# Counting edges with (destination, source parity) on the partitions: narrower one-hots, three-byte unpacking and another ScalarE order

## The chip, the cores and the metric

The kernel runs on one core of a Trainium2 chip. The metric is the device time of one execution in microseconds (us). Engines are named as in the profile: PE is TensorE's matmul side, PEld its weight loads, DVE VectorE, ACT ScalarE, POOL GpSimd, SP SyncE, which here only issues DMAs. A name with a q (DVEq) is the sequencer of an engine: it works on registers and semaphores and passes instructions on to the engine.

## The reference

A graph network over 6250 nodes and 100,000 edges sorted by destination, and then an expert FFN:

```python
n = x.shape[0]
deg = segment_sum(ones(rows.shape), rows, num_segments=n) + 1.0
dinv = rsqrt(deg)[:, None]
h = x @ W_in + b_in                      # x here is the layernorm of the input, 6250 x 256
for l in range(4):
    h_scaled = h * dinv
    msg = segment_sum(h_scaled[cols], rows, num_segments=n) * dinv
    global_ctx = mean(h, axis=0) @ Wg[l] + bg[l]
    z = relu((h + msg) @ Wl[l] + bl[l] + global_ctx)
    h = (z - mean(z)) * rsqrt(var(z) + EPS) * gamma[l] + beta[l]
...
x = x + h;  x = x + ffn(layernorm(x))    # top 2 of 8 experts
```

## The kernel before

The nodes lie in T = 49 tiles of 128. The edges are never gathered: the kernel first builds the dense matrix of edge counts (49 x 49 blocks of 128 x 128, as fp8) and writes it to HBM; each of the four layers then multiplies it with the node table. Building the matrix is the **counting stage**, the only one that the change touches. It goes through 49 **columns** m, one for each tile of 128 destinations. The edges lie in blocks of 128, sorted by destination, so a column needs only a window of WIN = 18 blocks.

For one column the engines do this:

- DVE writes one **source one-hot** for each block (`hots`, L724): a row of WP = 540 values for each edge, 49 tiles x 11 lanes, holding at the right place a power of four (which of 12 groups of 11 sources the edge falls in, so that one count word packs 12 two-bit counts). Two columns share 35 of them. It also writes the **destination one-hots** of the next column in one instruction (`hot_rows`, L708; `relative`, L699 and L700, prepares them from a start that is loaded into a register), the layernorm statistics of one tile of x (L731 to L747), and, once ACT has extracted the count words of the column before, the four **masks** that split them into two-bit fields (`mask`, L757).
- PE multiplies destination and source one-hots (`counts`, L1286, in two halves of 270 since 540 exceed one PSUM bank), and in between for the column before: `turn` (transpose of the normalised x tile), `product` (times W_in), `degrees` (49 matmuls of one column over the unpacked bytes, L1266) and `add_mean` (L1310).
- ACT copies the transposed tile (xnT, L1108), **unpacks** the masks into fp8 bytes with 12 ACTIVATEs (L1094), normalises the next x tile (xnb, L1112), stores h0 (L1100) and copies the count **words** out of PSUM (L1118).
- SP writes four finished columns at a time to HBM.

Each engine runs its list strictly in order; semaphores join them. Count words have two PSUM banks each and two buffers, the masks one. All names with `tab`, `later` and `region` in the profile are views of three big SBUF buffers.

## Time and profile before

| | us |
|---|---|
| median of 3 runs (3206.35 to 3207.5) | 3206.64 |
| the profiled execution | 3210.56 |
| its span, first to last instruction | 3208.6 |
| busy: PE / DVE / ACT / POOL | 3076.7 / 1901.3 / 855.9 / 70.3 |
| mean granted TensorE clock | 0.975 |

The span has five parts: setup (0 to 40 us), the counting stage (40 to 506), a change-over in which the counts are checked and the node table is made (506 to 563), the four layers (563 to 2806) and the FFN (2806 to the end). An engine's busy share says nothing by itself, since the stages are bound differently.

### The profile page before, as it was taken

Reading aid. Unit: us, or ns where it says so; the run is one execution under the profiler, and the core shown is the slowest. Engines: PE = TensorE matmul, PEld = TensorE weight load, DVE = VectorE, ACT = ScalarE, POOL = GpSimd, SP = SyncE. Lnnn points to the kernel's source line nnn. Section 1 sums busy time; section 2 is a strip of 40 time slices with the busy share of each in tenths; the row PEclk is TensorE's granted clock in tenths of the full one; section 3 lists DMA queues with packets and bytes.
Section 4 is the critical chain, followed back from the end, with each engine's and each line's share of the span. In section 5 each row is a group of like instructions: output and inputs, shape, how many; then the busy total and the mean of one; then the engine's idle time right before and its main releaser. Section 6 shows DMA issues by size and latency. Waiting matters only on the chain.

```text
span 3208.6 us, 54202 instructions
## 1 busy us (share of the span) xinstructions
PE 3076.7 (96%) x17323; PEld 1804.0 (56%) x17323; DVE 1901.3 (59%) x5185; ACT 855.9 (27%) x1934; POOL 70.3 (2%) x168
## 2 busy tenths in 40 slices
PE   6999996999999999999999999999999999979998
PEld 4777773444444444444444444444444444468887
DVE  8999997555555545555554555555566666645554
ACT  4989896111111111111111111111111111132332
POOL 0000000000000000000000000000000000001010
PEclk9989996999999999999999999999999999989999
DMA  4323324122222222222222222222222222110000
GB/s 130 96 83 94 91 82 122 61 70 70 70 70 70 70 70 70 70 70 70 70 70 70 70 70 70 70 70 70 80 82 82 82 82 82 48 40 16 18 18 18
DMA packets 134110, 225.11 MB, mean 70 GB/s; under 512 B 12277, under 2 KB 106596, under 8 KB 134018
## 3 DMA queue, kind: packets, MB, share of 16 engines
q1 hardware_dynamic: 131666, 217.53, 20.9%
q0 software_dynamic: 2352, 6.40, 0.8%
q8 instruction: 52, 0.85, 0.1%
q14 instruction: 40, 0.33, 0.0%
HBM read 178.17 MB, written 45.74 MB: 70 GB/s over the span
## 4 chain that ended last, share of the span: by engine, by line
PE 84%; ACT 9%; DVE 3%; issue 2%; DMA 1%; SPq 0%; DVEq 0%; ACTq 0%; POOLq 0%; POOL 0%
PE bank L1416 64%; ACT tab L1094 7%; PE bank L1490 5%; PE bank L1496 5%; PE bank L1374 4%; PE bank L1364 1%; PE bank L1266 1%; PE bank L1286 1%; DVE later L757 1%; DMA tab<-in_x 1%; DVE region L724 1%; PE bank L1310 1%; ACT later L1118 0%; PE bank L1304 0%; ACT xnb L1112 0%
## 5 line engine op out<-in xcount | busy, mean ns | idle before, releaser
L1416 PE MATMUL bank<-tab,region 128*128 128x512 f16 x9604 | 2143.2, 380 | 14.3 <-DVE tab L840 14.0
L1416 PEld LDWEIGHTS bank<-tab,region 128*128 128x128 fp8e4 x9604 | 940.8, 98 | 1065.5 <-DVE tab L840 17.9
L1094 ACT ACTIVATE tab<-later 128x539 fp8e4<-128x539 uint8 x588 | 336.1, 674 | 1.9 <-DVE later L757 1.9
L724 DVE TENSOR_SCALAR region<-iota_w,src_col,src_w 128x540 bf16<-128x540 int16 x858 | 310.8, 415 | 0.4 <-issue 0.3
L941 DVE SCALAR_TENSOR_TENSOR region<-bank,c_back,later 128x256 f32<-128x256 f32 x196 | 94.8, 484 | 351.2 <-PE bank L1374 351.2
L1197 ACT ACTIVATE sd<-mv,eps_c 128x1 f32<-128x1 f32 x196 | 57.8, 295 | 817.6 <-DVE mv L948 817.6
L936 DVE TENSOR_TENSOR region<-bank,region 128x256 f16<-128x256 f32 x196 | 83.3, 425 | 287.7 <-ACT region L1193 287.7
L1193 ACT ACTIVATE region<-bank 128x256 f16<-128x256 f32 x196 | 75.3, 384 | 568.2 <-PE bank L1364 568.2
L1490 PE MATMUL bank<-tab 128*128 128x384 f32 (+1 forms) x544 | 178.0, 487 | 3.8 <-DMA b_s<-in_L_ffn_b 3.8
L1496 PE MATMUL bank<-tab 128*128 128x256 f32 (+1 forms) x784 | 175.5, 384 | 0.9 <-ACT tab L1221 0.9
L1490 PEld LDWEIGHTS bank<-tab 128*128 128x128 f32 x544 | 164.4, 310 | 13.4 <-issue 6.3
L1374 PE MATMUL bank<-later,region 128*128 128x256 f16 x1176 | 161.0, 273 | 0.9 <-DVE region L936 0.9
L1496 PEld LDWEIGHTS bank<-tab 128*128 128x128 f32 (+1 forms) x784 | 148.8, 192 | 22.3 <-ACT tab L1221 1.4
L1191 ACT ACTIVATE region<-bank 128x256 f32<-128x256 f32 x196 | 75.3, 384 | 294.0 <-PE bank L1416 294.0
L1161 ACT ACTIVATE tab<-region,c_write 128x256 f32 x147 | 74.6, 508 | 274.1 <-DVE region L957 274.1
L1374 PEld LDWEIGHTS bank<-later,region 128*128 128x128 f16 x1176 | 115.2, 98 | 56.3 <-DVE region L936 1.2
L1221 ACT ACTIVATE tab<-bank,b_s 128x384 f32<-128x384 f32 (+1 forms) x136 | 77.2, 568 | 249.3 <-PE bank L1490 249.3
L1286 PE MATMUL bank<-region 128*128 128x270 bf16 x900 | 131.0, 299 | 1.3 <-DVE region L708 0.8
L1286 PE MATMUL bank<-region,later 128*128 x864 | 129.3, 309 | 1.4 <-DVE region L724 1.4
L925 DVE TENSOR_TENSOR region<-bank,region 128x256 f32<-128x256 f32 x196 | 83.0, 423 | 73.9 <-ACT region L1191 73.9
L1286 PEld LDWEIGHTS bank<-region,later 128*128 128x128 f16 x864 | 112.7, 145 | 15.4 <-issue 2.5
L1286 PEld LDWEIGHTS bank<-region 128*128 128x128 f16 x900 | 108.7, 146 | 19.9 <-DVE region L724 1.8
(199 smaller groups left out, 2232.8 us busy)
## 6 DMA issues: line engine op xcount, KB each, us to landing
region<-adjacency SPq DMA_DIRECT2D x196, 784.0 KB, 4.3
adjacency<-tab SPq DMA_DIRECT2D x12, 3136.0 KB, 13.7
region<-in_x POOLq DMA_DIRECT2D x48, 128.0 KB, 2.3
out<-region SPq DMA_DIRECT2D x48, 128.0 KB, 1.7
tab<-in_x SPq DMA_DIRECT2D x1, 6016.0 KB
tab<-in_L_ffn_W SPq DMA_DIRECT2D x4, 512.0 KB, 4.7
region<-in_L_gnn_Wl SPq DMA_DIRECT2D x1, 1024.0 KB, 5.4
later<-in_L_gnn_Wg SPq DMA_DIRECT2D x1, 1024.0 KB, 9.4
```

The costliest lines, as they stand in the source:

```text
L724: v.tensor_scalar(hot_s[:, j, :], iota_w[:, 0:WP], src_col[:, ds(first_block[0] + j, 1)], src_w[:, ds(first_block[0] + j, 1)], ALU.is_equa ...
L925: tile_own.done(v.tensor_tensor(acc_s, acc[a][:, 0:D], lo_f[:, a, :], ALU.add))
L936: v.tensor_tensor(uT[:, 1, :, :], T3[3], uT[:, 0, :, :], ALU.subtract).then_inc(uT_split, 1)
L941: tile_own.done(v.scalar_tensor_tensor(out=Z, in0=bank[4][:, 0:D], scalar=c_back[:, ds(n, 1)], in1=bias[:], op0=ALU.mult, op1=ALU.add))
L1094: ins = a.activation(stage[h][:, :, slot, f * LANES:f * LANES + n], counts[:, :, 0:n], ACT.Copy, saturate=False)
L1191: a.activation(lo_f[:, s, :], acc[s][:, D:2 * D], ACT.Copy).then_inc(lo_ready, 1)
L1221: a.activation(gT[:, f, 0:w], bank[f % 3][:, 0:w], ACT.Gelu, bias=b1_s[:, f // FC, f % FC:f % FC + 1]).then_inc(gelu_done, 1)
L1286: ins = mm(bank[k % 2 * 2 + half][:, 0:HALFP], hot_d[m % 2][:, :, j], hot_s[:, block + j, half * HALFP:(half + 1) * HALFP], start=j == 0, ...
L1374: ins = mm(bank[4][:, 0:D], uT[:, a, k, :], Wx[:, b, l, k, :], start=q == 0, stop=q == len(parts) - 1)
L1416: ins = mm(acc[a][:, :], A_s[:, a, m, :], tab[:, here + m, :], start=m == 0, stop=m == T - 1)
L1490: ins = mm(bank[f % 3][:, 0:w], W1_s[:, f // FC * KC + k, f % FC:FF:FC], xfT[:, k, 0:w], start=k == 0, stop=k == KC - 1)
L1496: ins = mm(bank[5 + u][0:r, 0:D], gT[:, f, u * P:u * P + r], W2_s[:, f // FC, f % FC, :], start=f == 0, stop=f == TOP * FC - 1)
```

## The change

A tile of 128 partitions of a count block now stands for 64 destinations times the parity of the source's tile (partition 2 x (destination in the half tile) + parity). A source one-hot therefore distinguishes 25 tile pairs instead of 49 tiles: 276 values instead of 540. A column is counted as two parts e = 0, 1 of 64 destinations each with a window of 10 blocks (20 matmuls of 275 instead of 36 of 270); four parts (two columns) form a group that shares 35 one-hots, as before. The destination one-hots grow from 18 to 20 blocks. `relative` loads two starts instead of one. The masks cover 1100 values instead of 1080. The unpacking takes three bytes in one ACTIVATE (five instead of twelve, 6400 elements instead of 6272). ACT works one column at once (words, xnT, root, normalise the next tile, unpack 0 and 1, h0, unpack 2 and 3), statistics are made two tiles ahead and their root and reciprocal for two tiles at a time, `degrees` comes two columns behind, and the masks follow the fourth one-hot of a column instead of the seventh. SP writes a group of columns with four DMAs of half the partitions and half the tiles. Words, masks and destination one-hots moved from `later` to `region`; the layer weights got buffers of their own. In the diff the old bodies of functions that are printed above are left out.

```diff
-WIN = 18
-STEP_LO, STEP_HI = 13, 17
-SLOTS = STEP_HI + WIN
-PAIRS = T // 2
-COLS = -(-NB // WIN) * WIN
+HALF_WIN = 10
+WIN = 2 * HALF_WIN
+HP = P // 2
+GROUP = 4
+GROUPS = -(-2 * T // GROUP)
+STEP_LO, STEP_HI = -2, 1
+STEP = HP * NE // (N * P)
+SLOTS = (GROUP - 1) * STEP + STEP_HI + HALF_WIN
+COLS = -(-(NB + SLOTS - HALF_WIN) // WIN) * WIN
...
-HALFP = WP // 2
+TI = -(-T // 2)
+WP = TI * LANES
+WS = -(-WP // 4) * 4
...
+words_w = work(4 * WP)
+words = words_w.bitcast(I32).rearrange("p (a s) -> p a s", a=2)
+words16 = words_w.bitcast(U16).rearrange("p (a s) -> p a s", a=2)
+masked_w = work(8 * WP)
+masked8 = masked_w.bitcast(U8).rearrange("p (k q s b) -> p k q b s", k=4, s=LANES, b=4)
...
-    sp.dma_start(X[:, 0, :], x[0:P, :]).then_inc(x0_in, 16)
-    sp.dma_start(X[:, 1:T - 1, :], x[P:(T - 1) * P, :].rearrange("(t p) f -> p t f", p=P)).then_inc(x_in, 16)
+    sp.dma_start(X[:, 0:2, :], x[0:2 * P, :].rearrange("(t p) f -> p t f", p=P)).then_inc(x0_in, 16)
+    sp.dma_start(X[:, 2:T - 1, :], x[2 * P:(T - 1) * P, :].rearrange("(t p) f -> p t f", p=P)).then_inc(x_in, 16)
...
     def write(h, m0, width):
         sp.wait_ge(staged, m0 + width + 1)
-        sp.dma_start(A[:, :, ds(m0, width), :].rearrange("t p m s -> p t (m s)"),
-                     stage32[h][:, :, 0:width, :].rearrange("p t m s -> p t (m s)")).then_inc(a_written[h], 16)
+        for odd in range(2):
+            n = TI - odd
+            for e in range(2):
+                sp.dma_start(A[odd::2, e * HP:(e + 1) * HP, ds(m0, width), :].rearrange("t p m s -> p t (m s)"),
+                             stage32[h][odd::2, e * TI:e * TI + n, 0:width * P // 4]).then_inc(a_written[h], 16)
...
+    def freed(g, slot):
+        lows = [0] + [i * STEP + STEP_LO for i in range(1, GROUP)]
+        i = max(i for i in range(GROUP) if lows[i] <= slot)
+        return (g - 1) * GROUP * HALF_WIN + i * HALF_WIN + min(slot - lows[i], HALF_WIN - 1) + 1
     def relative(m):
-        start = dve.value_load(starts[0:1, m:m + 1], min_val=0, max_val=COLS - WIN)
+        if m > 1:
+            dve.wait_ge(hot_d_ready, m - 1)
+        for e in range(2):
+            start = dve.value_load(starts[0:1, 2 * m + e:2 * m + e + 1], min_val=0, max_val=COLS - HALF_WIN)
+            ins = v.tensor_scalar(drel[m % 2][:, e * HALF_WIN:(e + 1) * HALF_WIN], dstf[:, ds(start, HALF_WIN)],
+                                  tile_base[:, 2 * m + e:2 * m + e + 1], None, ALU.subtract)
+        ins.then_inc(drel_ready, 1)
     def hot_rows(m):
...
+    def spread(m):
+        dve.wait_ge(x_in if m > 1 else x0_in, 32 if m > 1 else 16)
+        if m:
+            dve.wait_ge(xvar_ready, m)
+        if m >= 4:
+            dve.wait_ge(xscale_ready, m // 2 - 1)
+        v.bn_stats(xst[:], X[:, m, :]).then_inc(xst_ready, 1)
+    def moments(m):
+        hold(dve, xst_ready, m + 1)
+        v.bn_aggr(xmv[:, m // 2 % 2, m % 2, :], xst[:]).then_inc(xvar_ready, 1)
+    def inverse(g):
+        n = min(2, T - 2 * g)
+        dve.wait_ge(xstd_ready, g + 1)
+        if g > 1:
+            dve.wait_ge(xn_ready, 2 * g - 2)
+        v.reciprocal(xrs[:, g % 2, 0:n], xsd[:, 0:n]).then_inc(xrs_ready, 1)
+    def centre(g):
+        n = min(2, T - 2 * g)
+        dve.wait_ge(xrs_ready, g + 1)
+        v.scalar_tensor_tensor(out=xnb_bias[:, g % 2, 0:n], in0=xmv[:, g % 2, 0:n, 0], scalar=-1.0,
+                               in1=xrs[:, g % 2, 0:n], op0=ALU.mult, op1=ALU.mult).then_inc(xscale_ready, 1)
     first_block = [None]
     def hots(m, k, i):
+        g, second = m // 2, m % 2
+        split = STEP + STEP_HI + HALF_WIN
+        if not second:
+            first_block[0] = dve.value_load(starts[0:1, GROUP * g:GROUP * g + 1], min_val=0, max_val=NB)
         if m == 0:
             relative(0)
+        for at, j in enumerate(range(split, SLOTS) if second else range(split)):
+            if g:
+                dve.wait_ge(hot_used, freed(g, j))
+            v.tensor_scalar(hot_s[:, j, :], iota_w[:, 0:WS], src_col[:, ds(first_block[0] + j, 1)],
                             src_w[:, ds(first_block[0] + j, 1)], ALU.is_equal, ALU.mult).then_inc(hot_ready, 1)
             if m == 0 and at == 0:
                 hot_rows(0)
+            if m == 0 and at in (1, 3):
+                spread(at // 2)
+            if m == 0 and at in (2, 4):
+                moments(at // 2 - 1)
+            if m == 0 and at == 8:
+                inverse(0)
+            if m == 0 and at == 9:
+                centre(0)
+            if k and at == 3:
                 mask(m - 1, (k - 1) % 2)
+            if m + 2 < T and at == (5 if m else 10):
+                spread(m + 2)
+            if m + 2 < T and at == (6 if m else 11):
+                moments(m + 2)
             if m < T - 1 and at == 9:
                 relative(m + 1)
+            if second and at == 11:
+                inverse(g + 1)
             if m < T - 1 and at == 12:
                 hot_rows(m + 1)
+            if second and at == 13:
+                centre(g + 1)
     def mask(m, a):
...
+    def unpack(m, shifts):
+        k = (m - 1) % (2 * MG) + 1 if m else 0
+        i = (m - 1) // (2 * MG) if m else 0
         h, slot = k // MG % 2, k % MG
+        if shifts[0] == 0 and slot == 0:
+            act.wait_ge(a_written[h], AW * (i + k // (2 * MG) + 1))
             act.wait_ge(deg_done, m + 1)
+        for f in shifts:
+            at = slot * P + f * LANES
+            last = f == 3
+            lift = 3 * LANES if slot == MG - 1 and not last else 0
+            bytes_in = PARTS // 4 - last
+            hold(act, masks_ready, m * 4 + f + 1)
+            lanes = stage[h][:, :, at - lift:at - lift + bytes_in * 4 * LANES].rearrange("p q (b z) -> p q b z", b=bytes_in)
+            ins = a.activation(lanes[:, :, :, lift:lift + LANES], masked8[:, f, :, 0:bytes_in, :], ACT.Copy,
                                saturate=False)
+            if last:
+                n = P - 11 * LANES
+                ins = a.activation(stage[h][:, :, at + 8 * LANES:at + 8 * LANES + n], masked8[:, f, :, 2, 0:n],
+                                   ACT.Copy, saturate=False)
+        if last:
+            ins.then_inc(staged, 1)
     def h0(t):
         hold(act, in_mm, t + 1)
         a.activation(X[:, t, :], bank[7][:, 0:D], ACT.Copy).then_inc(h0_ready, 1)
+    def root_of(g):
+        n = min(2, T - 2 * g)
+        act.wait_ge(xvar_ready, min(2 * g + 2, T))
+        a.activation(xsd[:, 0:n], xmv[:, g % 2, 0:n, 1], ACT.Sqrt, bias=eps_c[:]).then_inc(xstd_ready, 1)
+    def normal(m):
+        hold(act, xscale_ready, m // 2 + 1)
+        a.activation(xnb[:], X[:, m, :], ACT.Identity, scale=xrs[:, m // 2 % 2, m % 2:m % 2 + 1],
+                     bias=xnb_bias[:, m // 2 % 2, m % 2:m % 2 + 1]).then_inc(xn_ready, 1)
+    def extract(m):
         act.wait_ge(hot_used, (m + 1) * WIN)
+        for e in range(2):
+            ins = a.activation(words[:, m % 2, e * WP:(e + 1) * WP], bank[m % 2 * 2 + e][:, 0:WP], ACT.Copy)
         ins.then_inc(words_ready, 1)
+        act.wait_ge(xnT_done, m + 1)
+        a.activation(xnT[:], T3[4], ACT.Copy).then_inc(xnT_copied, 1)
+        if m % 2 == 0 and m + 2 < T:
+            root_of(m // 2 + 1)
+        if m + 1 < T:
+            normal(m + 1)
+        unpack(m, (0, 1))
+        h0(m)
+        unpack(m, (2, 3))
+    root_of(0)
+    normal(0)
+    for m in range(T):
+        extract(m)
...
+    def degrees(m):
+        k = (m - 1) % (2 * MG) + 1 if m else 0
         h, slot = k // MG % 2, k % MG
         hold(pe, staged, m + 2)
+        for q in range(2 * TI):
+            i = q % TI
+            ins = mm(bank[6][:, 2 * i:2 * i + 2], stage[h][:, q, slot * P:(slot + 1) * P], odd_b[:], start=False,
+                     stop=False)
         ins.then_inc(deg_done, 1)
     def counts(m, k, i):
         if k:
             pe.wait_ge(words_ready, m)
+        for e in range(2):
+            g, part = m // 2, m % 2 * 2 + e
+            block = 0
+            if part:
+                at = g * (GROUP - 1) + part - 1
+                block = pe.value_load(steps[0:1, at:at + 1], min_val=part * STEP + STEP_LO,
+                                      max_val=part * STEP + STEP_HI)
+            ready = g * SLOTS + (part * STEP + STEP_HI if part else 0)
+            for j in range(HALF_WIN):
+                if k and e * HALF_WIN + j == TURN_AT:
+                    turn(m - 1)
+                if k and e * HALF_WIN + j == PRODUCT_AT:
+                    product(m - 1)
+                if e == 0 and j == 0:
+                    pe.wait_ge(hot_d_ready, m + 1)
+                pe.wait_ge(hot_ready, ready + j + 1)
+                mm(bank[k % 2 * 2 + e][:, 0:WP], hot_d[m % 2][:, :, e * HALF_WIN + j], hot_s[:, block + j, 0:WP],
+                   start=j == 0, stop=j == HALF_WIN - 1).then_inc(hot_used, 1)
+        if m > 1:
+            degrees(m - 2)
         if k:
             add_mean(m - 1, mean_w)
...
-    degrees(T - 1, 2 * MG)
     product(T - 1)
+    degrees(T - 2)
+    degrees(T - 1)
```

Three pieces of the engines' lists follow, with the waits on semaphores. First DVE, in the middle of the stage, from the masks of a column to the destination one-hots; "ISA" is a register instruction of the sequencer. Before:

```order
L757 TENSOR_SCALAR later<-later 128x1080 [waits staged,words_ready]
L757 TENSOR_SCALAR later<-later 128x1080 x3
L724 ISA
L724 TENSOR_SCALAR region<-iota_w,src_col,src_w 128x540
...
L699 TENSOR_LOAD starts
L699 ISA x2
L700 ISA
L700 TENSOR_SCALAR drel<-dstf,tile_base 128x18
...
L708 TENSOR_TENSOR region<-rep,drel 128x2304 [waits drel_ready,hot_used]
```

Now:

```order
L807 TENSOR_SCALAR region<-region 128x1100 [waits staged,words_ready]
L807 TENSOR_SCALAR region<-region 128x1100 x3
...
L741 BN_STATS xst<-tab 128x6 [waits xscale_ready,xvar_ready,x_in]
...
L746 BN_AGGR xmv<-xst 128x2 [waits xst_ready]
...
L721 TENSOR_LOAD starts [waits hot_d_ready]
L721 ISA x2
L722 ISA
L722 TENSOR_SCALAR drel<-dstf,tile_base 128x10
L721 TENSOR_LOAD starts
...
L731 TENSOR_TENSOR region<-rep,drel 128x2560 [waits drel_ready,hot_used]
```

The statistics moved from the start of a column to behind the masks (two one-hots after them), and two loads with their register work stand between the masks and the destination one-hots, where one stood.

Then PE, from the last counting matmul of a column to the first of the next. Before:

```order
L1286 MATMUL bank<-region,later 128x270
L1266 MATMUL bank<-one_b,tab 128x1 [waits staged]
L1266 MATMUL bank<-one_b,tab 128x1 x48
L1310 MATMUL bank<-tab,mean_w 128x256 [waits h0_ready]
L1297 MATMUL bank<-ident,xnb 128x128 [waits xn_ready,words_ready]
```

Now:

```order
L1363 MATMUL bank<-region 128x275
L1339 MATMUL bank<-odd_b,tab 128x2 [waits staged]
L1339 MATMUL bank<-odd_b,tab 128x2 x49
L1386 MATMUL bank<-tab,mean_w 128x256 [waits h0_ready]
L1373 MATMUL bank<-ident,xnb 128x128 [waits xn_ready,words_ready]
```

The list reads alike; what moved is the column that `degrees` waits for, m - 2 instead of m - 1. The transposes still stand behind the last counting matmul of the column.

Last ACT, one column. Before:

```order
L1118 ACTIVATE later<-bank 128x270 [waits hot_used]
L1118 ACTIVATE later<-bank 128x270
L1105 ACTIVATE xsd<-xmv,eps_c 128x1 [waits xvar_ready]
L1108 ACTIVATE xnT<-bank 128x256 [waits xnT_done]
L1094 ACTIVATE tab<-later 128x49x11 [waits masks_ready]
...
L1112 ACTIVATE xnb<-tab,xnb_bias,xrs 128x256 [waits xscale_ready]
L1100 ACTIVATE tab<-bank 128x256 [waits in_mm]
```

Now:

```order
L1182 ACTIVATE region<-bank 128x275 [waits hot_used]
L1182 ACTIVATE region<-bank 128x275
L1185 ACTIVATE xnT<-bank 128x256 [waits xnT_done]
L1171 ACTIVATE xsd<-xmv,eps_c 128x2 [waits xvar_ready]
L1175 ACTIVATE xnb<-tab,xnb_bias,xrs 128x256 [waits xscale_ready]
L1155 ACTIVATE tab<-region 128x50x3x11 [waits masks_ready] x2
L1166 ACTIVATE tab<-bank 128x256 [waits in_mm]
L1155 ACTIVATE tab<-region 128x50x3x11 [waits masks_ready]
L1155 ACTIVATE tab<-region 128x50x2x11 [waits masks_ready]
L1159 ACTIVATE tab<-region 128x50x7
```

Before, the words of column m came out behind the unpacking of column m - 1, and its transposed tile and its unpacking belonged to the next round; in both orders xnT of a tile stands between the words of a column and the unpacking.

## Rows read from the trace of the kernel before

**Rows 1.** The page: span, and busy us of the engines.

```profile
span 3208.6 us, 54202 instructions
PE 3076.7 (96%) x17323; PEld 1804.0 (56%) x17323; DVE 1901.3 (59%) x5185; ACT 855.9 (27%) x1934; POOL 70.3 (2%) x168
```

**Rows 2.** Windows by stage: length, busy us (instructions) per engine, PEclk, DMA share, GB/s.

```profile
40.00:506.00 466.00, 429.22 (x4553) 352.88 (x4553) 443.14 (x1316) 415.33 (x865) 0.00 (x0) 0.92 0.28 78
506.00:563.00 57.00, 28.99 (x134) 14.23 (x133) 41.94 (x102) 30.42 (x71) 1.85 (x3) 0.59 0.58 166
563.00:2806.00 2243.00, 2238.33 (x11136) 1100.64 (x11135) 1188.71 (x3170) 291.99 (x784) 24.78 (x46) 1.00 0.21 71
```

**Rows 3.** Waits, 40 to 506 us: total us, times, longest.

```profile
ACT xnT L1108 <- PE bank L1297: 46.2, 47, 1.6
PE bank L1266 <- ACT tab L1094: 36.6, 38, 1.4
```

**Rows 4.** Timeline of one column: start, length, instruction, idle before it.

```profile
474.81 1.36 PE L1266 MATMUL bank<-one_b,tab 128*128 128x1 bf16 x49 [1.12 <-ACT tab L1094]
475.32 0.65 ACT L1118 ACTIVATE later<-bank 128x270 int32<-128x270 f32 x2
476.01 1.49 DVE L757 TENSOR_SCALAR later<-later 128x1080 uint16<-128x1080 uint16 x4 [0.64 <-ACT later L1118]
476.97 0.39 ACT L1108 ACTIVATE xnT<-bank 128x256 f32<-128x256 f32 x1 [0.81 <-PE bank L1297]
477.25 6.86 ACT L1094 ACTIVATE tab<-later 128x539 fp8e4<-128x539 uint8 x12
479.73 1.35 DVE L708 TENSOR_TENSOR later<-rep,drel 128x2304 f16<-128x2304 f16 x1
481.00 2.40 DVE L724 TENSOR_SCALAR region<-iota_w,src_col,src_w 128x540 bf16<-128x540 int16 x7
```

**Rows 5.** Windows: two columns after each other, columns as in rows 2.

```profile
474.80:484.20 9.40, 8.43 (x95) 6.86 (x95) 8.76 (x27) 8.59 (x19) 0.00 (x0) 1.00 0.27 75
484.20:494.40 10.20, 9.41 (x95) 7.82 (x95) 10.20 (x31) 8.62 (x19) 0.00 (x0) 0.83 0.01 2
```

**Rows 6.** Groups by line and shape, DVE: busy us, mean ns, idle before.

```profile
L724 DVE TENSOR_SCALAR region<-iota_w,src_col,src_w 128x540 bf16<-128x540 int16 x858 | 310.8, 415 | 0.4 <-issue 0.3
L952 DVE TENSOR_SCALAR region<-region,mv,rs 128x256 f32<-128x256 f32 x196 | 80.8, 412 | 7.1
L757 DVE TENSOR_SCALAR later<-later 128x1080 uint16<-128x1080 uint16 x196 | 73.1, 437 | 22.6 <-ACT later L1118 22.2
L944 DVE TENSOR_SCALAR region<-region 128x256 f32<-128x256 f32 x196 | 57.6, 294 | 6.8
```

**Rows 7.** Lines L699 and L724, DVE's sequencer: ns min/median/max, first to last start.

```profile
L699 DVEq TENSOR_LOAD <-starts x49: 301/313/946, 25.7 to 485.9; - x49
L724 DVEq FUSED_REGOPS  x6: 69/69/69, 29.6 to 30.4; - x6
```

**Rows 8.** Timeline where the stage starts.

```profile
26.41 0.24 DVE L700 TENSOR_SCALAR drel<-dstf,tile_base 128x18 f16 x1 [1.72 <-issue]
28.51 0.42 DVE L731 BATCH_NORM_STATS2 xst<-tab 128x6 f32<-128x256 f32 x1
29.61 1.08 DVE L724 TENSOR_SCALAR region<-iota_w,src_col,src_w 128x540 bf16<-128x540 int16 x3 [0.26 <-issue]
38.94 0.43 DVE L731 BATCH_NORM_STATS2 xst<-tab 128x6 f32<-128x256 f32 x1 [2.02 <-DMA tab<-in_x]
```

**Rows 9.** Line L1118, the count words, two for each of 49 columns.

```profile
L1118 ACT ACTIVATE later<-bank x98: 368/383/412, 36.8 to 504.7; 128x270 int32<-128x270 f32 x98
```

**Rows 10.** End of the stage: transposes with a register load before them, bytes of the last column, node table.

```profile
467.03 0.20 PEld L1297 LDWEIGHTS bank<-ident,xnb 128*128 128x128 f32 x2 [0.44 <-issue]
505.71 6.85 ACT L1094 ACTIVATE tab<-later 128x539 fp8e4<-128x539 uint8 x12 [0.65 <-DVE later L757]
523.45 19.65 ACT L1170 ACTIVATE tab<-tab,c_write  x49 [1.47 <-DVEq L826]
```

223 lines of the change are left out of this document (78 added, 145 removed).

## The prediction

> **What bounds the kernel now.** I read the page first, then the windows by stage. The span is 3208.6 us [rows 1]. The four layers take 2243 us with PE busy for 2238 [rows 2]; the change moves no instruction there, so they stay. The counting stage takes 466 us, and there no engine is full: PE is busy 429 us, DVE 443, ACT 415 [rows 2]. A stage that three engines share so evenly is bound by how they wait for each other, so I read the waits next. The longest is ACT's, for the transposed x tile (46.2 us in 47 waits), then PE's `degrees` matmuls for ACT's unpacking (36.6 us) [rows 3].
>
> The timeline of one column shows the circle. PE's 49 small matmuls start at 474.81, released by the last unpacking; `add_mean` and the transposes follow, ACT takes xnT at 476.97, 2.2 us later, and unpacks for 6.86 us [rows 4]; then the next 49 may start. That is 9.4 us a column, of which ACT works 8.59 and DVE 8.76 [rows 5]. The words come first at 36.8 us and last at 504.7, or 504.4 for the first of that pair [rows 9]: 467.6 us for 48 columns, 9.74 each. The gap between 9.4 and 9.74 is mostly TensorE's clock. The column from 474.80 had it at 2.4 GHz throughout and took 9.40 us; the next had a granted clock of 0.83, so a part of it at 1.2 GHz, and took 10.20 [rows 5]. Before that fall PE had stood idle 1.0 to 1.1 us and issued one-column matmuls for 1.4 [rows 4].
>
> **What the change removes.** `degrees` two columns behind takes that circle apart: the unpacking it waits for ended a column earlier. ACT alone would then need 8.6 us: its 8.59 of now [rows 5], with one root in place of two in each pair of columns (-0.1) and 6400 elements in place of 6272 (6.86 x 1.02, +0.1 [rows 4]). PE's matmuls fall from 36 to 20 and cost the sum nothing, since others set the column.
>
> The one-hots on DVE are half as wide, but not half as long. The rows give a price for width and for scalars. With 256 f32 elements a TENSOR_SCALAR without a per-partition scalar takes 294 ns, with two of them 412 [rows 6]: 118 ns for two scalars, whatever the width. The masks (1080 16-bit elements, no such scalar) take 437 ns; the one-hot (540, two scalars) 415, or 297 without them [rows 6]. So 540 elements cost 140 ns and 264 fewer save 69. The pitch of now is (2.40 - 0.415) / 6 = 0.331 us [rows 4], that of the new one-hot 0.26. The bounds are 0.331 (nothing saved) and 0.169 (in proportion to the width); I take 0.26, because it follows from two groups of the same operation. The saving is 1.2 us of DVE time a column. Against it stand 0.14 us for longer destination one-hots (1.27 x 20/18; 1.27 is 481.00 less 479.73 [rows 4]) and a second `relative`.
>
> **What takes the circle's place.** Since all lists run in order, a new one closes: words of m-1, masks of m-1, one-hots of m, counting matmuls of m, `degrees`, `add_mean` and transposes, xnT of m, unpacking of m, words of m+1. It spans two columns. For an even m, from the start of the words:
>
> - 0.69 to the masks (475.32 to 476.01 [rows 4]).
> - Masks 1.45, two one-hots 0.52, statistics 0.42 [rows 8]: 2.4 us, and there the sequencer holds for the statistics.
> - A hold empties the queue. At 29.61 the one-hot behind the same hold waited 0.26 us for issue [rows 8]. The sequencer needs 0.15 us for each one-hot (six register steps from 29.6 to 30.4 [rows 7]), so three one-hots and the aggregation bring it to the first load 0.65 us after the hold. A load is 0.31 us [rows 7] and with its register work 0.8: two cost 1.72 us of idle DVE when nothing covered them [rows 8]. So the one-hot after them starts 0.65 + 1.6 + 0.1 = 2.35 us behind the hold, at 4.75. The engine's own work to there would be 1.3 us, so about 1.0 us is stall. Now one load stands three one-hots and the whole masks behind the last hold, and is covered by them.
> - Three one-hots 0.79, destination one-hots 1.41, six one-hots 1.31 plus the last one's own 0.35: the last is written at 8.6. PE needs that last one for its last matmul.
> - 0.3 to that matmul and past it, then from the first small matmul to xnT 2.2 (474.81 to 476.97 [rows 4]), and 0.3 more for an even m, whose transposes stand behind a register load as at 467.03 (0.44 [rows 10]).
> - ACT without the words: 8.6 - 0.6, and 0.1 for the root: 8.1.
>
> The sum is 0.69 + 8.6 + 0.3 + 2.5 + 8.1 = 20.2 us for two columns, 10.1 each. An odd m has three one-hots fewer, 0.2 us more of small steps, no load before the transposes and no root, 18.9; it is the faster of two chains that share one pace, and has 1.3 us to spare. So I get 10.1 us a column at 2.4 GHz. Behind the waiting xnT on ACT stand the whole unpacking and the next words; ACT will idle about 1.3 us a column.
>
> The clock adds something. While the destination one-hots are made, PE has nothing to count, then works at DVE's pace, then does the small matmuls: about 4 us with little in them, where it now has some 2.4. A column with a fall costs 0.8 us now [rows 5], and about one in three has one (0.3 us a column between 9.4 and 9.74). With more falls, but the odd chain's slack taking some, I add 0.15 us.
>
> The Trainium skill (TensorE: Matmul & The Clock Gate, the section on HAM oscillation) ties the fall to PE standing idle between bursts, and asks only for no long gap. By that rule the clock would stay up, in both kernels, and the added 7 us would be zero. The trace does not agree: the clock fell with PE busy 8.43 of 9.40 us in the column before [rows 5].
>
> **Ends of the stage.** At the start, the statistics of tile 2 now stand in column 0 and wait for the whole x, which lands at 38.94 [rows 8]; then come two one-hots, the destination one-hots and six more, 3.9 us. The first words move from 36.8 to 43, and the next two follow at 9 us each. Then 46 columns at 10.1 end at 43.2 + 18 + 464.6 = 525.8, less 0.8 since the last word belongs to the faster chain: 525, against 504.4, so +20.6. At the end, the product of the last tile no longer follows `degrees`, which saves about 3.7 us of the path to the scales; but the last bytes (ready at 512.6) must also land, the node table starts at 523.45 [rows 10], and the unpacking ends 0.8 later after the words. I take -1.5. The fourfold DMAs I cost at nothing: the stage's DMA share is 0.28 [rows 2], and each write has four columns of cover.
>
> Sum: +20.6 + 7 - 1.5 = +26 us. Against the profile's own execution (3210.56, span 3208.6) that is 3236.6; the median lies 3.9 lower, so 3206.64 + 26 = 3232.7, and I say 3232.
>
> **The rivals.** *ACT becomes the bound.* If the sequencer ran far enough ahead and the one-hots fell to 0.17 us, the new circle would be 1.0 + 11 x 0.09 = 2.0 us shorter, 9.1 a column, and with xnT earlier it approaches ACT's 8.6. At 8.6 to 9.1 the stage loses 30 to 50 us, and with the later start the time is 3160 to 3185; at 9.4, 3195. The point that decides is 9.55 us a column. For it: the halved width, and that ACT's present wait goes. Against it: the two scalars' 118 ns, and the hold in front of two loads. In all 0.2.
>
> *The loads stay hidden.* Then the circle is 19.2, 9.6 a column, and the time about 3208 with the clock's share: no change that can be measured. The same page of the Trainium skill (its opening table) gives VectorE's queue eight places in strict order. By that rule a full queue would cover both loads, eight one-hots at 0.26 being 2.1 us against 1.6. The row against it is the stall of 0.26 us right behind a hold [rows 8], as the queue is not full there. 0.13.
>
> *The clock stays at 1.2 GHz most of the time.* Then the 2.5 us of `add_mean` and transposes grow by 1 us and the product becomes late for h0: about 10.7 a column, 3255 and more. 0.07.
>
> *The one-hots don't get faster at all* (0.331): 0.8 us more in the circle, +18 us, 3250. It is in the forecast's range.
>
> **How the numbers follow.** My forecast, 3212 to 3255, has 0.6. The range is 3190 to 3256: it takes in the hidden loads and a part of ACT's case. A measurement of this kernel tells 0.2%, or 6.4 us, from no change. Faster by more than that: 0.2; within it: 0.13; slower: 0.67.
>
> **What would show it.** In the new profile: the words 20 us later at the end and about 10.1 us apart; new one-hots of 0.34 us; DVE idle with "issue" as its releaser before the second `relative` and after it, 1 us a column; DVE waiting for ACT's words about 1 us; ACT waiting for PE's transposes about as long as now. The forecast is wrong if ACT is busy over 95% of the stage, or if the issue stall is missing.

## The result: 1.8% slower, more than twice the loss that was forecast

The changed kernel takes 3264.15 us (median; 3263.08 to 3267.75), the kernel before in the same runs 3206.49: a ratio of 1.0181, 95% interval 1.0164 to 1.0199. That is +58 us where +26 was forecast, and outside the range of 3190 to 3256. The direction is right, the size is not.

The page of the changed kernel, span and busy us, answers to [rows 1]:

```profile
span 3265.9 us, 52717 instructions
PE 3085.9 (94%) x16588; PEld 1755.7 (54%) x16588; DVE 1865.7 (57%) x5192; ACT 838.1 (26%) x1567; POOL 69.4 (2%) x170
```

Every engine but PE has less to do, and the span grew. The windows of the changed kernel, by stage and then of two neighbouring columns (columns as in [rows 2] and [rows 5]):

```profile
40.00:562.00 522.00, 443.31 (x3800) 307.84 (x3799) 407.83 (x1320) 398.79 (x506) 0.00 (x0) 0.74 0.24 69
562.00:619.00 57.00, 27.38 (x179) 15.12 (x180) 41.72 (x102) 30.68 (x66) 1.88 (x3) 0.62 0.58 172
619.00:2861.00 2242.00, 2238.97 (x11136) 1100.69 (x11133) 1187.68 (x3168) 290.88 (x782) 24.71 (x46) 1.00 0.21 71
303.80:314.60 10.80, 7.38 (x63) 5.04 (x61) 7.92 (x27) 8.41 (x12) 0.00 (x0) 0.94 0.84 241
292.90:303.80 10.90, 9.58 (x66) 6.09 (x65) 8.82 (x28) 8.06 (x11) 0.00 (x0) 0.53 0.01 2
```

The layers are as long as before. All of the difference lies in the counting stage, where the granted clock fell from 0.92 to 0.74. The two columns, of an even and an odd m, are about equally long, but not for the same reason: the first has the clock almost throughout, the second hardly. The starts of the words are 43.5 us for m = 0 and 561.7 for the last. From m = 2 to m = 45 the step after an even m is 10.83 us in the mean, and after an odd m 10.92 (the last two steps, 8.54 and 9.33, are left out).

The longest waits of the changed kernel, 40 to 562 us, in total us, times and longest:

```profile
PEld bank L1363 <- issue: 97.6, 139, 1.8
PE bank L1363 <- DVE region L775: 78.8, 77, 3.3
DVE region L807 <- ACT region L1182: 59.0, 48, 1.9
DVE drel L722 <- issue: 50.6, 92, 1.3
ACT xsd L1171 <- DVE xmv L746: 42.2, 23, 2.6
ACT xnT L1185 <- PE bank L1373: 39.3, 36, 2.1
ACT tab L1166 <- PE bank L1380: 37.2, 20, 2.8
```

Two of these the prediction did not have. ACT's square root (L1171) waits for the statistics in 23 columns, and ACT's copy h0 (L1166) for the product in 20. Here is the even column in the timeline (start, length, instruction, idle before it):

```profile
303.88 0.67 ACT L1182 ACTIVATE region<-bank 128x275 int32<-128x275 f32 x2
304.58 1.51 DVE L807 TENSOR_SCALAR region<-region 128x1100 uint16<-128x1100 uint16 x4 [1.40 <-ACT region L1182]
306.01 0.61 DVE L775 TENSOR_SCALAR region<-iota_w,src_col,src_w 128x276 bf16<-128x276 int16 x2
306.53 0.42 DVE L741 BATCH_NORM_STATS2 xst<-tab 128x6 f32<-128x256 f32 x1
307.12 0.17 DVE L746 BATCH_NORM_AGGREGATE xmv<-xst 128x2 f32<-128x6 f32 x1
307.33 0.29 ACT L1171 ACTIVATE xsd<-xmv,eps_c 128x2 f32<-128x2 f32 x1 [1.87 <-DVE xmv L746]
307.53 0.58 ACT L1175 ACTIVATE xnb<-tab,xnb_bias,xrs 128x256 f32<-128x256 f32 x1
308.02 3.27 ACT L1155 ACTIVATE tab<-region 128x1650 fp8e4<-128x1650 uint8 x2
308.98 0.23 DVE L722 TENSOR_SCALAR drel<-dstf,tile_base 128x10 f16 x1 [0.90 <-issue]
310.42 0.23 DVE L722 TENSOR_SCALAR drel<-dstf,tile_base 128x10 f16 x1 [1.21 <-issue]
311.10 0.92 PE L1363 MATMUL bank<-region 128*128 x3 [1.13 <-DVE region L775]
313.35 1.04 PE L1363 MATMUL bank<-region 128*128 x3 [1.32 <-DVE region L775]
314.66 0.66 ACT L1182 ACTIVATE region<-bank 128x275 int32<-128x275 f32 x2
```

The reader is to see a circle within one column. ACT writes the words and comes to the root 3.45 us later (307.33 less 303.88), because the root takes the variance of tile m+3, whose statistics stand in DVE's list behind the masks, and those wait for these same words. Behind the root ACT works without a pause to the next words at 314.66: 3.45 + 7.33 = 10.78. Nothing of TensorE is in it. Two other even columns bear this out, the first with the clock low for more than half of the time and hardly a DMA, the second with the clock high and the DMA engines 87% busy:

```profile
325.81:336.60 10.79, 8.44 (x81) 5.99 (x80) 8.16 (x27) 8.29 (x12) 0.00 (x0) 0.71 0.01 2
347.56:358.34 10.78, 7.36 (x63) 5.02 (x60) 7.94 (x27) 8.39 (x12) 0.00 (x0) 0.97 0.87 245
```

So neither the clock nor the fourfold writes lengthen an even column. The odd column before the first one:

```profile
292.92 0.67 ACT L1182 ACTIVATE region<-bank 128x275 int32<-128x275 f32 x2
293.62 1.52 DVE L807 TENSOR_SCALAR region<-region 128x1100 uint16<-128x1100 uint16 x4 [1.88 <-ACT region L1182]
296.25 0.87 DVE L775 TENSOR_SCALAR region<-iota_w,src_col,src_w 128x276 bf16<-128x276 int16 x3
297.05 1.22 PE L1378 MATMUL bank<-bin_s,ones 1*128 1x256 f32 x2
298.19 2.08 PE L1380 MATMUL bank<-Win_s,xnT 128*128 128x256 f32 x4
300.37 0.38 ACT L1166 ACTIVATE tab<-bank 128x256 f32<-128x256 f32 x1 [2.84 <-PE bank L1380]
```

The product stands behind counting block 7 of the next column, four one-hots after the masks, and at 1.2 GHz takes 3.3 us from its start to h0. ACT stands 2.84 us in the middle of its unpacking. This is a second circle, and the clock is part of it. The odd column from 97.84 us, with more of the clock, is 0.8 us shorter:

```profile
97.84:107.95 10.11, 8.73 (x74) 5.92 (x71) 8.51 (x28) 8.23 (x11) 0.00 (x0) 0.83 0.23 65
```

### The profile page after: what moved, and what is told of

The parts are those of the page before. It is cut to its first block, busy times and chain, and to the rows that moved or that the text cites. A ratio compares the mean times of both kernels' runs of the same rounds, so it can differ in the third digit from the quotient of the medians.

```text
span 3265.9 us, 52717 instructions
## 1 busy us (share of the span) xinstructions
PE 3085.9 (94%) x16588; PEld 1755.7 (54%) x16588; DVE 1865.7 (57%) x5192; ACT 838.1 (26%) x1567; POOL 69.4 (2%) x170
## 3 DMA queue, kind: packets, MB, share of 16 engines
q1 hardware_dynamic: 132290, 217.53, 20.4%
## 4 chain that ended last, share of the span: by engine, by line
PE 89%; DVE 3%; ACT 3%; issue 2%; DVEq 1%; DMA 1%; SPq 1%; ACTq 0%; POOLq 0%; POOL 0%
PE bank L1493 63%; PE bank L1567 5%; PE bank L1573 5%; PE bank L1363 4%; PE bank L1451 4%; PE bank L1380 2%; PE bank L1339 1%; ACT tab L1155 1%; PE bank L1441 1%; DVE region L775 1%; PE bank L1386 1%; PE bank L1378 1%; DVE region L807 1%; DMA tab<-in_x 1%; DVEq L721 0%
## 5 line engine op out<-in xcount | busy, mean ns | idle before, releaser
L1363 PE MATMUL bank<-region 128*128 (+1 forms) x980 | 236.3, 376 | 83.3 <-DVE region L775 79.3
L1155 ACT ACTIVATE tab<-region 128x1650 fp8e4<-128x1650 uint8 x196 | 304.6, 1612 | 0.4 <-DVE region L807 0.4
L998 DVE SCALAR_TENSOR_TENSOR region<-bank,c_back,bias 128x256 f32<-128x256 f32 x196 | 94.8, 483 | 351.2 <-PE bank L1451 351.2
L775 DVE TENSOR_SCALAR region<-iota_w,src_col,src_w 128x276 bf16<-128x276 int16 x859 | 248.6, 346 | 0.8 <-issue 0.8
L1363 PEld LDWEIGHTS bank<-region 128*128 128x128 f16 x980 | 147.1, 155 | 170.3 <-issue 102.8
L1451 PE MATMUL bank<-Wx,region 128*128 128x256 f16 x1176 | 160.8, 273 | 0.9 <-DVE region L993 0.9
L1451 PEld LDWEIGHTS bank<-Wx,region 128*128 128x128 f16 x1176 | 115.1, 98 | 56.1 <-DVE region L993 1.2
L897 DVE SCALAR_TENSOR_TENSOR tab<-region,c_write,tab 128x256 f32 x147 | 71.2, 484 | 73.0 <-ACT tab L1232 73.0
L807 DVE TENSOR_SCALAR region<-region 128x1100 uint16<-128x1100 uint16 x196 | 74.2, 442 | 62.9 <-ACT region L1182 62.9
```

What stands on the lines that cost most here:

```text
L775: v.tensor_scalar(hot_s[:, j, :], iota_w[:, 0:WS], src_col[:, ds(first_block[0] + j, 1)], src_w[:, ds(first_block[0] + j, 1)], ALU.is_equa ...
L807: v.tensor_scalar(masked16[:, s, :], words16[:, a, :], 2 * s, 0x0303, ALU.logical_shift_right, ALU.bitwise_and).then_inc(masks_ready, 1)
L998: tile_own.done(v.scalar_tensor_tensor(out=Z, in0=bank[4][:, 0:D], scalar=c_back[:, ds(n, 1)], in1=bias[:], op0=ALU.mult, op1=ALU.add))
L1155: ins = a.activation(lanes[:, :, :, lift:lift + LANES], masked8[:, f, :, 0:bytes_in, :], ACT.Copy, saturate=False)
L1363: mm(bank[k % 2 * 2 + e][:, 0:WP], hot_d[m % 2][:, :, e * HALF_WIN + j], hot_s[:, block + j, 0:WP], start=j == 0, stop=j == HALF_WIN - 1). ...
L1451: ins = mm(bank[4][:, 0:D], uT[:, a, k, :], Wx[:, b, l, k, :], start=q == 0, stop=q == len(parts) - 1)
```

## The experiments

Times are medians; each ratio is to the kernel before in runs on the same chip.

### The two circles, one at a time

Statistics ahead of the masks:

```diff
-                    if m + 2 < T and at == (5 if m else 10):
+                    if m + 2 < T and at == (1 if m else 10):
                         spread(m + 2)
-                    if m + 2 < T and at == (6 if m else 11):
+                    if m + 2 < T and at == (2 if m else 11):
                         moments(m + 2)
```

> The changed kernel with the statistics of tile m+3 (BN_STATS and moments) moved in VectorE's list of column m+1 from behind the masks of column m to behind one-hots 1 and 2, ahead of them. Theory A (root circle: after an even column's words ScalarE's square root waits for statistics that stand behind the masks, which wait for the same words; 40.1 us over 22 columns in the profile after): the wait of the root on the moments falls from 40.1 us to under 8, even columns fall from 10.8 us to 9.3 to 10.1, and the time falls by 12 to 30 us, to about 3240 us. Theory B (the path runs by TensorE's late product in every column, and the root's wait only replaces the wait of the product behind it): the root's wait goes, but the wait of h0's copy on the product grows by as much in the even columns, and the time stays within 6 us of 3264. Theory C (the circle of masks and loads over two columns that the prediction named): as B, within 10 us.

3207.8 us, ratio 0.9997 (0.9986 to 1.0008): 56.4 us less, more than the upper end of what theory A said. Steps after an even m fell from 10.83 to 9.02 us, after an odd m from 10.92 to 10.10 (these means, too, are of m = 2 to 45). Its waits, 60 to 520 us; the line of the root is gone and the issue stall, 45.9 us in the changed kernel in this window, is under a quarter:

```profile
DVE region L807 <- ACT region L1182: 52.0, 44, 5.1
ACT tab L1166 <- PE bank L1380: 33.0, 25, 2.7
DVE drel L722 <- issue: 10.0, 20, 0.9
```

Relative numbers ahead of the masks (`relative(m + 1)` at one-hot 2 instead of 9):

> The changed kernel with the relative numbers of column m+1 (two register loads, two subtractions) moved in VectorE's list from behind one-hot 9 to behind one-hot 2, ahead of the masks. The stall in which VectorE waits for its own issue (49.1 us over 88 instructions) then falls into the time in which it would wait for the words. Theory A (root circle in even columns, late product in odd ones): the stall is behind the root's release in even columns, and in odd ones it delays the one-hots and so the product, so only odd columns gain, 0.5 to 1 us each: 12 to 24 us in all, about 3247 us. Theory C (the prediction's circle, in which the whole stall is on the path in every column): 1 us a column, 45 us, about 3220 us. Theory D (the stall is hidden by waits anyway): within 6 us of 3264.

3268.0 us, ratio 1.0189 (1.0172 to 1.0206). The stall fell from 45.9 us to 15.4 (60 to 520 us) and nothing came of it: DVE waited for the words instead, 92.5 us for 52.2. Theory D holds in the time. The move also made ACT's wait for the product longer (62.3 us for 36.2), so it is not a pure test of the stall; what it shows is that taking the stall away gave nothing as long as the two circles stood.

h0's copy at the end of the unpacking:

```diff
                 unpack(m, (0, 1))
-                h0(m)
                 unpack(m, (2, 3))
+                h0(m)
```

> The changed kernel with ScalarE's copy of the input product (h0) moved from the middle of the unpacking to its end. Theory A (in odd columns the copy waits for a product that TensorE reaches late; 36.2 us over 19 columns): the wait falls under 10 us, odd columns fall from 10.96 us to 10.1 or 10.3, the even ones stay at 10.8 by the root, and the time falls by 12 to 20 us, to about 3248 us. Rival (the copy's release late in the column holds TensorE's mean behind it, and the product's wait only moves): within 6 us of 3264, and a wait of TensorE on h0 of over 20 us appears.

3243.6 us, ratio 1.0110 (1.0093 to 1.0127): 20.6 us less. After an odd m 9.98 us, after an even m still 10.84, as the root circle demands. The product ahead of counting block 4 (`PRODUCT_AT` 8 to 4) tests the same circle from TensorE's side:

> The changed kernel with TensorE's product of the last tile ahead of counting block 4 of a column in place of block 8, so that it no longer waits for one-hots that stand behind the masks. Nothing changes on ScalarE and VectorE. Theory B (odd columns wait for the late product): odd columns fall from 10.9 us to 10.0 to 10.2, even ones stay at 10.8 by the root, 3240 to 3247 us, as with h0's copy moved. Rival (h0's copy was late for another reason): within 6 us of 3264.

3243.2 us, ratio 1.0111 (1.0093 to 1.0129), steps of 10.84 and 9.87. Two different edits of the odd circle give the same 21 us, and neither moves the even columns.

All three moves, and then without the loads':

> All three moves together: statistics and relative numbers ahead of the masks, h0's copy behind the unpacking. Theory A: both circles are gone, a column is bound by ScalarE's 8.6 us plus some 0.5 us or by VectorE's one-hots, 9.0 to 9.5 us, over 46 columns 60 to 80 us less than after: 3184 to 3205 us, at or below the kernel before. Theory clock (the columns are long because TensorE's clock stands at 1.2 GHz more than half of the time, and what waits is a consequence): under 20 us less, over 3244 us, with a granted clock that stays at 0.74 in the stage.

> Early statistics and h0's copy behind the unpacking, relative numbers where the change has them. All three moves together were 14.6 us slower than the early statistics alone. If the copy's place is to blame (TensorE's mean at the end of a column then waits for it, 36.9 us over 35 waits in that run): 3215 to 3225 us. If the place of the relative numbers ahead of the masks is to blame (stall of 64.2 us for VectorE's own issue, against 10.0): 3195 to 3208 us, as h0's wait of 33.0 us falls away.

3222.4 (1.0046, 1.0030 to 1.0063) and 3202.0 us (0.9982, 0.9973 to 0.9992). Neither theory for all three was right: moving the loads cost 20.4 us there. They stood right behind the hold (a wait on which the sequencer itself stands, here for the statistics), and the stall rose to 64.2 us over 88 waits, while DVE hardly waited for words any more (5.4 us). With statistics and hold ahead of the masks and the loads behind them, DVE waits for the words, its sequencer runs ahead in that time, and the loads are covered. In the run with the early statistics the masks start at 274.69 us, the two loads at 275.7 and 277.1, and the first instruction that needs a load at 277.69, without idle time:

```profile
L721 DVEq TENSOR_LOAD <-starts x2: 864/896/927, 275.7 to 277.1; - x2
```

Early statistics and early product:

> Early statistics (3207.8 us) and the early product. If the two circles account for the miss, both are gone: the columns fall from a mean of 9.56 us to 9.0 to 9.4, 3180 to 3200 us. If the low clock (0.78 in that run) is what is left, the product's place gives little: 3200 to 3210 us.

3197.6 us, ratio 0.9965 (0.9952 to 0.9978), a mean step of 9.39 us. With both circles gone the changed kernel is just ahead of the one before.

### What else the early statistics gave

The root moved behind `unpack(m, (0, 1))`, DVE's list as in the change:

> The changed kernel with VectorE's list untouched; ScalarE's square root for the next pair of tiles moves from ahead of normalise and unpack to behind the first half of the unpacking (it is needed only in the next column). Theory A (what costs is that ScalarE stands still at the root until the statistics behind the masks are done): even columns fall from 10.8 us to about 9 as in the run with the early statistics, and the time falls by 40 to 56 us, to 3208 to 3225 us. Rival (the early statistics helped by what they gave VectorE, fewer issue waits and work in the idle time before the masks, not by releasing ScalarE): even columns fall by under 0.5 us, time over 3250 us.

3245.5 us, ratio 1.0117 (1.0100 to 1.0134): 18.7 us less, where theory A said 40 to 56. So releasing ACT is not all that the early statistics do. Short and long columns stood side by side, 9.1 and 11.4 us; the mean after an even m fell only to 10.20. Two runs on the rest:

> The root moved behind the first half of the unpacking (3245.5 us) and the relative numbers ahead of the masks. What the early statistics gave beyond the later root (38 us) is either VectorE's stall for its own issue (45.9 us over 84 instructions with the later root, 10.0 over 20 with the early statistics) or something else. Theory stall: the time falls by 20 to 40 us, to 3205 to 3225 us. Theory clock (columns are long in which TensorE runs at 1.2 GHz, and the order on VectorE matters only through the waits that it gives TensorE): within 10 us of 3245.

> The root moved behind the first half of the unpacking, and the eight added matmuls a column that nobody reads. In the run without them columns of 9.1 and of 11.4 us stood side by side, with the product at 0.69 + 1.13 us in the short ones and 1.22 + 2.07 us in the long ones. Theory clock: the granted clock of the stage rises from 0.75 to over 0.85, the long columns thin out, and the time falls by 20 to 45 us, to 3200 to 3225 us. Theory stall (VectorE's issue stall sets the column): within 8 us of 3245.

The first took 3232.8 us (1.0082, 1.0065 to 1.0099), 12.7 less; the second 3249.2 (1.0128, 1.0112 to 1.0145), 3.7 more, with a granted clock of 0.82. So moving the loads is worth something once the root is out of the way, but less than theory stall said, and the added matmuls bought nothing here. Of the 56.4 us, the later root alone gave 18.7 and the loads on top of it 12.7; 25 are left. The columns tell where they are. With the later root and the early loads an even m takes 8.81 us in the mean (down to 8.5 in columns at 2.4 GHz, about ACT's own work), less than the 9.02 of the early statistics. So in the even columns the root and the loads together are the whole account. The rest lies in the odd ones, at 11.54 us against 10.10, where ACT waits 49.1 us for the product instead of 27.9 (60 to 500 us). Why the product comes later there was not taken apart.

### The clock

Eight more matmuls a column, which nobody reads:

```diff
                            start=j == 0, stop=j == HALF_WIN - 1).then_inc(hot_used, 1)
+                        if k and e == 0 and j < PRODUCT_AT:
+                            mm(bank[6][:, 256:512], rep[:, :, 0], rep[:, 0:16, 0:16], start=False, stop=False)
```

> The changed kernel with eight more matmuls a column (256 columns each, into an unused part of a bank, read by nobody) behind counting blocks 0 to 7, while TensorE would wait for one-hots. If they hold the granted clock near 1.0, the transposes and the product take 1.8 us in place of 3.3 in each column. Theory A (even columns wait for statistics, odd ones for the product): even columns stay at 10.8 us, odd ones fall from 10.96 to 9.6 to 10.2 us, the time by 17 to 30 us, to about 3240. Theory clock (the low clock makes all columns long): both kinds fall and the time by 40 us or more. If the clock stays at 0.74, the added work shows its own price instead: up to 8 us of TensorE's waits used up, time within 10 us of 3264.

3261.0 us, ratio 1.0168 (1.0151 to 1.0185): the clock rose only to 0.81 (60 to 500 us). Even columns stayed at 10.8 us but for one of 11.9, odd ones spread from 9.7 to 12.8. Windows of such two, and the product in the first:

```profile
75.80:85.50 9.70, 8.55 (x47) 5.98 (x46) 8.31 (x27) 8.15 (x11) 0.00 (x0) 0.79 0.00 1
223.30:236.10 12.80, 12.80 (x127) 9.69 (x125) 9.05 (x29) 8.28 (x12) 0.00 (x0) 0.60 0.15 42
```

```profile
80.18 0.69 PE L1380 MATMUL bank<-bin_s,ones 1*128 1x256 f32 x2
80.81 1.13 PE L1382 MATMUL bank<-Win_s,xnT 128*128 128x256 f32 x4
82.03 0.39 ACT L1166 ACTIVATE tab<-bank 128x256 f32<-128x256 f32 x1 [1.00 <-PE bank L1382]
```

In the first the clock rose just ahead of the product. From its start to h0 it took 1.85 us, not 3.32, and the column is 1.2 us shorter than the odd one above. With the 0.8 us between two odd columns of the changed kernel, that makes 0.8 to 1.2 us as the clock's price in an odd column. In the second the clock stayed low until the product was done. There each added matmul lasts 0.42 us and not 0.27, a counting matmul and an added one start every 0.44 us and not every 0.23, and PE is full. The edit helps only where it raises the clock.

With the early statistics, and with h0's copy last too:

> The early statistics (3207.8 us) and the added matmuls together. Theory A: the even columns' wait is gone already, the odd ones (10.1 us, with ScalarE's wait for the product of 33.0 us over 25 columns) fall by 0.7 to 1.2 us when the clock is held at 2.4 GHz, to about 3185 us. If the clock is not raised, or is low only because TensorE waits: 3205 to 3215 us.

> Early statistics, h0's copy last and the added matmuls, with the degrees where the change has them. With the runs of early statistics and h0's copy last (3202.0), the same with the degrees in the middle (3240.1), and that with the added matmuls (3168.0) this fills the table. Theory 1 (the clock is the larger part): 3170 to 3185 us, so the degrees' place gives under 15 us once the clock is held. Theory 2 (the degrees' place is the larger part and needs the clock): 3190 to 3202 us.

3198.9 us (0.9977, 0.9967 to 0.9986) at a clock of 0.90, less gain than expected, since the odd columns fell to 9.47 us but the even ones rose to 9.40; and 3187.3 us (0.9940, 0.9923 to 0.9958) at 0.88, between the ranges of its two theories. The table is filled by two runs in which `degrees` and `add_mean` of column m-2 stand ahead of counting block 12 of column m, not behind the last block:

```diff
+                        if m > 1 and e * HALF_WIN + j == 12:
+                            degrees(m - 2)
+                            add_mean(m - 2, mean_w)
                         pe.wait_ge(hot_ready, ready + j + 1)
...
-                if m > 1:
-                    degrees(m - 2)
-                if k:
-                    add_mean(m - 1, mean_w)
```

> Early statistics and h0's copy last, and besides TensorE's degrees and mean of column m-2 stand ahead of counting block 12 of column m in place of behind its last one. ScalarE's wait of 51.7 us over 46 columns for the transposes (they stand behind degrees and mean, and those behind h0's copy) and TensorE's 30.5 us for h0 should fall to under 15 each. If the column is bound by that circle: 0.4 to 0.8 us a column, 3165 to 3185 us. If VectorE (428 us busy of 500) or TensorE at 1.2 GHz takes over as the bound: 3190 to 3202 us; slower than 3205 if the degrees in the middle delay the last counting blocks by more than they free.

> The run with the degrees in the middle and the eight added matmuls a column, which raised the granted clock of the stage from 0.76 to 0.87 in the run on the early statistics. If TensorE's path binds a column (transposes, product, degrees): 10 to 20 us below the run without the added matmuls. If VectorE binds it: the same time within 5 us, or up to 10 us slower, since the added matmuls hold back counting blocks.

3240.1 us (1.0107, 1.0090 to 1.0124) and **3168.0 us (0.9882, 0.9866 to 0.9898)**. The second is the fastest kernel of this study, 38.6 us below the kernel before. Their windows, first without the added matmuls, 60 to 500 us:

```profile
60.00:500.00 440.00, 374.88 (x3434) 276.84 (x3432) 353.07 (x1172) 348.14 (x451) 0.00 (x0) 0.74 0.27 78
```

and with them, 60 to 465 us since the last words of this run start at 465.7, where two columns follow:

```profile
60.00:465.00 405.00, 354.02 (x4108) 285.90 (x4106) 379.31 (x1261) 378.96 (x486) 0.00 (x0) 0.97 0.32 89
228.60:237.50 8.90, 7.67 (x89) 5.92 (x88) 8.90 (x31) 8.22 (x11) 0.00 (x0) 1.00 0.37 102
237.50:245.70 8.20, 7.30 (x90) 6.21 (x91) 8.07 (x29) 8.20 (x11) 0.00 (x0) 1.00 0.01 3
```

| Early statistics, h0 last | without added matmuls | with them |
|---|---|---|
| degrees behind the last block | 3202.0 us, clock 0.77 | 3187.3 us, clock 0.88 |
| degrees ahead of block 12 | 3240.1 us, clock 0.74 | 3168.0 us, clock 0.97 |

I expected the degrees' place to gain by itself, and the added matmuls to give 10 to 20 us on top of it. It lost 38 us at the low clock, as the last branch of its expectation had it, where ACT's wait of the words for the counting grew from 7.6 us to 91.9, and gained 19 at the high one. Now DVE fills one column of the pair (8.90 of 8.90 us) and ACT the other (8.20 of 8.20). Neither theory of the table's last run is the whole answer: the degrees' place pays only where the clock is held.

The fastest kernel with its statistics back behind the masks:

> The fastest kernel so far (3168.0 us: early statistics, h0's copy last, degrees in the middle, added matmuls) with its statistics put back behind the masks. Theory A (root circle): even columns return to 10.8 us whatever the clock, odd ones stay near 8.7 to 9.0 us; over 23 even columns 2.3 us each, so 3215 to 3225 us. Theory clock (with the clock held, the place of the statistics costs little, since the early statistics had helped by keeping TensorE busier): under 15 us more, below 3183 us.

3295.8 us (1.0279, 1.0261 to 1.0297), the slowest of all and 127.8 above the fastest. Its even columns are at 10.86 us, as the root circle says, with a clock of 0.89 in the one from 300.69 us. But the odd ones went to 12.2, which no expectation had. Its waits, 60 to 500 us:

```profile
ACT region L1182 <- PE bank L1366: 79.6, 19, 4.7
ACT xsd L1171 <- DVE xmv L746: 46.5, 19, 2.5
```

The stage's clock is 0.79 with the added matmuls in it. My reading is that the wait at the root gives TensorE a wait in the even column, the clock falls, and in the odd column the added matmuls and the degrees delay the counting: the even columns have a mean clock of 0.94 and the odd ones 0.67. No run takes this apart; this kernel without the added matmuls was not run.

### One part of the change alone

The kernel before, with `degrees` two columns behind:

```diff
-                if k:
-                    degrees(m - 1, k - 1)
-                    add_mean(m - 1, mean_w)
+                if m > 1:
+                    degrees(m - 2, (m - 3) % (2 * MG) + 1 if m > 2 else 0)
+                if k:
+                    add_mean(m - 1, mean_w)
```

> The kernel before with one part of the change alone: TensorE adds up the degrees of column m-2 behind the counts of column m, where it added those of m-1. The prediction's account of the kernel before (the circle of unpack, degrees, transposes and xnT binds its column at 9.4 us, and this part takes it apart): the wait of ScalarE's xnT on the transposes falls and a column comes to 8.6 to 9.1 us, the time to 3175 to 3195 us. Rival (the circle is as long through the counting blocks or VectorE's one-hots of 412 ns, 18 of them and the rest of its column): within 6 us of 3207.

3186.9 us, ratio 0.9942 (0.9926 to 0.9959). Wait and clock of that run, 60 to 500 and 60 to 480 us:

```profile
ACT xnT L1108 <- PE bank L1298: 17.9, 45, 1.0
```

```profile
60.00:480.00 420.00, 404.98 (x4309) 329.76 (x4309) 418.14 (x1252) 398.07 (x821) 0.00 (x0) 0.99 0.31 86
```

ACT's wait for the transposes, which [rows 3] have at 46.2 us, is 17.9, and the last words of the stage start 23 us earlier (481.5 us instead of 504.4). The column is 9.26 us (481.5 less 36.8, over 48), not the 8.6 to 9.1 of the expectation, bound by DVE, which is busy 418 of 420 us. The clock rose with it, from 0.92 to 0.99, so the gain is of both: in the kernel before, the column of [rows 5] that had the clock throughout took 9.40 us.

## Why the prediction missed, and what in it held

*What bounds the kernel before* was right: taking the circle apart gained 19.7 us by itself, though only until DVE was full. *The layers* did not move.

*The one-hots* were right. These are their group in the changed kernel, ten of them in a row, and the start:

```profile
L775 DVE TENSOR_SCALAR region<-iota_w,src_col,src_w 128x276 bf16<-128x276 int16 x859 | 248.6, 346 | 0.8 <-issue 0.8
```

```profile
38.86 0.43 DVE L741 BATCH_NORM_STATS2 xst<-tab 128x6 f32<-128x256 f32 x1 [3.05 <-DMA tab<-in_x]
41.21 2.70 DVE L775 TENSOR_SCALAR region<-iota_w,src_col,src_w 128x276 bf16<-128x276 int16 x10
```

(2.70 - 0.346) / 9 = 0.262 us of pitch, where 0.26 was worked out from the price of two scalars. *The start* was right too: first words at 43.5 us for 43.

*The new circle over two columns* is the step that failed. The prediction said "8.1" for ACT with "0.1 for the root" in it, and called the odd chain "the faster of two chains" with 1.3 us to spare. It had charged the root's work and never asked what the root waits for, though the statistics had just been moved behind the masks. And its sum had the product nowhere on the path; only a rival named it. So each column has a circle of its own, 10.78 and 10.96 us in place of 20.2 for the two. The sum by terms, in starts of words: first words +0.3 us against the 43.2 of the sum; two columns at the start +3.8 (21.8 for 18); 46 columns at 10.79 us in place of 10.1 + 0.15, +24.8; and the 0.8 that the sum took off for a last column of the faster chain, +0.8, as the mean of 10.79 has the short last steps in it. That makes 561.7 where 525 + 7 was forecast. Of the signs that the prediction listed only the pitch and the end of the words were off. The others could not have told the two circles from the forecast one: one-hots of 0.346 us, an issue stall of 50.6 us, DVE's wait for words (59.0) and ACT's for the transposes (39.3) all came about as it said.

*The issue stall* was right in size and place (50.6 us, 1.1 a column) and wrong as a term: with the loads moved the time did not fall, so other waits covered it. The rival in which the loads stay hidden did not come about in the change (0.90 and 1.21 us behind a hold) and does where the masks' wait stands between hold and loads (10.0 us in all). The Trainium skill (TensorE: Matmul & The Clock Gate, the opening table) gives VectorE's queue eight places in strict order. The traces agree with it: with the early statistics the first load starts at 275.7 us, while the third of the four masks runs, so with one mask and six one-hots between the two in the list, and it is covered. Right behind a hold the queue is empty and covers nothing.

*The clock* was the second step that failed, as a term: 0.15 us a column, where it costs an odd column 0.8 to 1.2 us and an even one, which took 10.8 us at clocks of 0.71 and of 0.97, nothing. That is 0.4 to 0.6 in the mean. The stage's clock is 0.74, so about half of the time was at 1.2 GHz. The rival to which I gave 0.07, the clock low and the product late for h0, is what happened in the odd columns; that its 10.7 us and 3255 are near is in part luck, as the even columns are long for a reason that it does not have. What PE did before the fall: in the even column above it waited 1.1 to 1.3 us at a time for one-hots, and it was at 1.2 GHz in the next. Between 60 and 500 us PE's matmuls are never idle for longer than 1.8 us, and the mean clock is 0.73. The Trainium skill (TensorE: Matmul & The Clock Gate, the section on a second failure mode, psum-queue depth-cycling) tells of another kernel in which small pauses between groups of matmuls were enough to make the clock swing. The trace agrees with that section, and not with a reading by which only a long gap counts. The same page of the Trainium skill (Loop structure matters more than you think) has the loop nest decide on the clock. Here two kernels with the same loops, apart from eight unread matmuls a column, were granted 0.74 and 0.97, so the nest alone does not decide it.

*The end* was wrong by 4 us. From the last words to the node table it is 21.6 us, and was 19.0. The timeline of ACT in the changed kernel:

```profile
578.96 0.24 ACT L1227 ACTIVATE root<-degp 128x49 f32<-128x49 f32 x1 [5.30 <-DVE degp L869]
583.29 16.86 ACT L1241 ACTIVATE tab<-tab,c_write  x42 [4.09 <-DMA adjacency<-tab]
```

The early product gained nothing there: from the last words to `root` it is 17.3 us in both kernels. And the table now waits for the last write, one of the fourfold DMAs that were costed at nothing: it lands at 582.96 us, 21.3 behind the last words, where the kernel before had its last write at 521.27, 16.9 behind.

What stays open: 25 of the 56 us that the early statistics gave, of which only the place is known, and why the degrees' place changes sign with the clock. For the second only the rows of the table are shown, the mechanism (the 50 matmuls of `degrees` and the two of `add_mean` ahead of the last counting blocks, at half the clock) is argued.
